# Expert weights and buffers laid over attention buffers in the order in which these die

## The reference

```python
# attention, per graph; 12 heads of 32
u = layernorm(x)
q, k, v = u @ Wq.T, u @ Wk.T, u @ Wv.T + bv
a = softmax(q @ k.T * 384**-0.5 + adj)            # rows that are all 0 are masked
x = x + (a @ v) @ Wo.T + bo
# experts, per graph; activations gelu, silu, mish, gelu
u = layernorm(x)
logits = u.mean(axis=1) @ router_w.T + router_b   # top 2 of 4, gates = softmax of the two
h = act_e(u @ w1[e] + b1[e])                      # 384 -> 768
y = sum(gate * (h @ w2[e] + b2[e])) + u
out = x + layernorm(y) * ln_g + ln_b
```

## Time and profile before

| | |
|---|---|
| median of 3 runs | 1660.82 us (1660.15 to 1662.0) |
| the profiled execution, its own time | 1659.58 us |
| its span, first to last instruction | 1657.8 us |
| PE busy | 1598.8 us, 96% |
| DVE, ACT, POOL busy | 71%, 58%, 50% |
| PE busy in the slices of 41 us from 663 and 705 us | 0.8 and 0.5 |
| DMA in the same two slices | 293 and 292 GB/s |

### The profile page before, as it was taken

One profiled execution on the slowest core, in us unless ns is written; L12 is line 12 of the kernel. 1 busy time (PEld: TensorE's weight loads), 2 busy tenths in 40 slices (PEclk: granted clock), 3 DMA queues, 4 the chain that ended last, 5 costly groups with the idle time before them and its releaser, 6 DMA issues.

```text
span 1657.8 us, 45212 instructions
## 1 busy us (share of the span) xinstructions
PE 1598.8 (96%) x12756; PEld 1533.7 (93%) x12757; DVE 1179.8 (71%) x3677; ACT 957.1 (58%) x2821; POOL 827.4 (50%) x1235
## 2 busy tenths in 40 slices
PE   8999999999999999859999999999999999999997
PEld 7999999999999999759999999999999999999997
DVE  5888888888888878737755665676677667566764
ACT  6899999999999988832422222333334323243431
POOL 4888888888888877612232333232323223322333
PEclk9999999999999999979999999999999999999999
DMA  6444443355555533872222222222221222222220
GB/s 194 144 141 140 133 141 128 136 173 171 179 178 172 175 127 124 293 292 63 63 73 72 71 72 72 72 72 72 72 72 57 64 71 70 72 72 72 72 69 33
DMA packets 93743, 188.19 MB, mean 114 GB/s; under 512 B 10336, under 2 KB 57440, under 8 KB 91872
## 3 DMA queue, kind: packets, MB, share of 16 engines
q1 hardware_dynamic: 91520, 169.39, 31.3%
q10 hardware_dynamic: 2016, 16.52, 2.7%
HBM read 108.80 MB, written 77.07 MB: 112 GB/s over the span
## 4 chain that ended last, share of the span: by engine, by line
PE 87%; DVE 5%; issue 3%; ACT 3%; POOL 1%; DMA 1%; DVEq 1%; ACTq 0%; POOLq 0%; SPq 0%
PE bank L423 67%; PE bank L497 5%; PE bank L622 4%; PE bank L450 3%; PE bank L520 3%; PE bank L537 2%; PE bank L529 1%; PE bank L506 1%; DVE half_t L1289 1%; DVE inverse L1296 1%; DVE inverse L1292 1%; ACT inverse L889 1%; ACT at_hi L856 1%; DMA ut_scratch<-ut_out 1%; DVE hid L1184 1%
## 5 line engine op out<-in xcount | busy, mean ns | idle before, releaser
L423 PE MATMUL bank<-w_hi,ut_in 128*128 x1536 | 423.8, 343 | 10.1 <-DVE hid L1184 8.9
L685 ACT ACTIVATE prob<-att,neg_max 128x128 f32<-128x128 f32 x768 | 297.3, 390 | 14.8 <-DVE neg_max L1044 11.2
L423 PEld LDWEIGHTS bank<-w_hi,ut_in 128*128 128x128 f32 x1536 | 281.5, 189 | 15.2 <-issue 15.0
L880 ACT ACTIVATE hid<-hid 128x384 f32<-128x384 f32 x192 | 95.1, 526 | 318.0 <-DVE hid L1184 305.2
L423 PE MATMUL bank<-w_hi,at_hi 128*128 x768 | 258.3, 336 | 5.0 <-DVE at_lo L1261 5.0
L1012 POOL TENSOR_SCALAR rs_z<-mv_z 128x1 f32<-128x1 f32 x64 | 14.7, 230 | 497.0 <-DVE mv_z L1315 450.0
L1261 DVE SCALAR_TENSOR_TENSOR at_lo<-bank,gate_col,at_hi 128x384 fp32r<-128x384 f32 x256 | 146.1, 612 | 162.9 <-ACT at_hi L856 162.9
L423 PE MATMUL bank<-w_lo,ut_in 128*128 x768 | 258.2, 336 | 0.0
L423 PE MATMUL bank<-w_hi,at_lo 128*128 x768 | 257.0, 335 | 0.0
L423 PE MATMUL bank<-w_lo,at_hi 128*128 x768 | 256.6, 334 | 0.0
L856 ACT ACTIVATE at_hi<-bank,gate_col 128x384 fp32r<-128x384 f32 x256 | 134.6, 577 | 170.0 <-PE bank L622 168.2
(11 more groups left out here) (135 smaller groups left out, 3826.5 us busy)
## 6 DMA issues: line engine op xcount, KB each, us to landing
xu_scratch<-xu SPq DMA_DIRECT2D x64, 384.0 KB, 2.3
ut_scratch<-ut_out SPq DMA_DIRECT2D x64, 384.0 KB, 2.7
ut_in<-ut_scratch SPq DMA_DIRECT2D x64, 384.0 KB, 3.0
xz<-xu_scratch SPq DMA_DIRECT2D x64, 384.0 KB, 3.1
x_in<-in_x SPq DMA_DIRECT2D x32, 384.0 KB, 4.9
xu<-in_x SPq DMA_DIRECT2D x32, 384.0 KB, 4.2
out_dram<-xz SPq DMA_DIRECT2D x64, 192.0 KB, 1.9
w_lo<-in_L_ffn_w SPq DMA_DIRECT2D x4, 1152.0 KB, 6.0
```

The lines of the kernel that those rows point to most:

```text
L423: last = nc.tensor.matmul(acc, lhs[c][a], rhs[c][b], start=start and n == 0, stop=stop and n == len(terms) - 1)
L685: nc.scalar.activation(prob[g][:, hh, :], att[g][:, head, :], ACT.Exp, bias=neg_max[g][:, head:head + 1], scale=-1.0, accum_out=row_sum[g] ...
L880: nc.scalar.activation(hid[k][:, s], hid[k][:, s], ACT.Gelu).then_inc(a_ready[k], 1)
```

## The change

SBUF is laid out anew. The attention buffers are allocated in an order in which those that die early lie under what is wanted early, and w2_lo and w2_hi become one region, w2_both, that lies exactly over a run of attention buffers: a filler, q and k of the even pairs, xt of the odd pairs, adj, q and k of the odd pairs, att0, prob0, att1, fold, prob1, pt, inv_t, inv_sum, and ot of both parities. The w2 scratch in HBM gets the same order within each partition, and eight transfers of unequal size take the place of eight equal ones of 2,304 columns. b1_wide and b2_wide change places in time: b1 is loaded in step 60 by ACT, and b2 only after attention, by SP, between the loads of xz0 and xz1.

Since other buffers now lie under hid, half_t, inverse and at_hi, the waits change too: ACT waits at the end of attention for the stores of xu0 and for the last output projection, no longer for the stores of xu1 and ut. DVE waits in step 65 for o_mm in place of xu_stored. And since b2 comes later, `add_output_bias` moves on DVE: for graph 0 to the end of (1, 0), for all other graphs to the end of their (b, k), behind `split_act_lo`, `activate_second` and `normalise_z`.

```diff
-    w2_dram = nc.dram_tensor("w2_scratch", (2, E, P, FC, D), F32, kind="Internal").ap()
+    w2_dram = nc.dram_tensor("w2_scratch", (P, 2, E, FC, D), F32, kind="Internal").ap()
...
-        w2_lo = sb("w2_lo", [P, E, FC, D], F32R)
-        w2_hi = sb("w2_hi", [P, E, FC, D], F32R)
         hid = [sb(f"hid{k}", [P, 2, HALF]) for k in range(K)]
-        half_t = sb("half_t", [P, 2, HALF])
+        w2_both = sb("w2_both", [P, 2, E, FC, D], F32R)
...
+        under = {}
+        edge = 0
+        for name, tiles in (("unused", (unused,)), ("qk0", (q_t[0], k_t[0])), ("xt1", (xt_hi[1], xt_lo[1])), ("adj", adj_in), ("qk1", (q_t[1], k_t[1])), ("att0", (att[0],)),
+                            ("prob0", (prob[0],)), ("att1", (att[1],)), ("fold", (fold,)), ("prob1", (prob[1],)),
+                            ("pt", pt), ("inv_t", (inv_t,)), ("inv_sum", inv_sum), ("ot0", (ot[0], ot_hi[0], ot_lo[0])),
+                            ("ot1", (ot[1], ot_hi[1], ot_lo[1]))):
+            width = sum(math.prod(tile[:].shape[1:]) for tile in tiles)
+            under[name] = (edge, edge + width)
+            edge += width
+        assert edge == 2 * E * FC * D
...
             load_xz(0, 0)
+            sp.dma_start(b2_wide[:].rearrange("p e d -> p (e d)"), b2.rearrange("(o e) d -> o (e d)", o=1).partition_broadcast(P)).then_inc(b2_loaded, 16)
             load_xz(1, 1)
...
-                            pe.wait_ge(w2_loaded, 32 * E)
+                            pe.wait_ge(w2_loaded, 16 * 8)
...
                 if h == B - 4:
                     act.wait_ge(xn_done, B)
-                    act.dma_start(b2_wide ...).then_inc(wide_loaded, 16)
+                    act.wait_ge(v_mm, B - 2)
                     act.wait_ge(qk_mm, 2 * B - 2)
+                    act.dma_start(b1_wide ...).then_inc(b1_loaded, 16)
                     load_w1_hi(1)
                 if h == B - 3:
                     act.wait_ge(qk_mm, 2 * B)
                     load_w1_hi(2)
+                    act.wait_ge(s_mm, B - 2)
+                    load_w2("unused", "qk0")
...
             def load_under_scores():
                 act.wait_ge(s_mm, B)
-                load_w2(0, 0)
                 act.wait_ge(exp_done, HEADS * (B - 1))
                 act.wait_ge(fold_done, FOLDS * (B - 1))
-                load_w2(0, 1)
+                act.wait_ge(pt_mm, PTC * (B - 1))
+                load_w2("qk1", "prob0")
...
             act.wait_ge(routed, 1)
             for g in range(2):
-                for p in range(2):
-                    act.wait_ge(xu_stored[p][g], 16 * (B // 4))
-                act.wait_ge(ut_stored[g], 16 * (B // 2))
+                act.wait_ge(xu_stored[0][g], 16 * (B // 4))
+            act.wait_ge(wo_mm, B)
...
                     if graph(b, 0):
                         activate_first(b, k, e)
-                        add_output_bias(b, k, m, lap, e)
...
                     if k == 0 and graph(b, -2):
                         normalise_z(b - 2, (m - 2) % 4)
+                    if isinstance(b, int) and (b, k) == (1, 0):
+                        dve.wait_ge(b2_loaded, 16)
+                        for first in range(K):
+                            add_output_bias(0, first, 0, 0, choice(0, first))
+                    if graph(b, 0) and not (isinstance(b, int) and b == 0):
+                        add_output_bias(b, k, m, lap, e)
```

113 lines of the change are left out of this document (60 added, 53 removed).

## The result

The changed kernel takes 1666.2 us in the median of 20 runs (1659.92 to 1670.76), the kernel before 1660.07 beside it (20 runs, 1657.37 to 1663.78). The ratio is 1.0032 with an interval from 1.0023 to 1.0041: slower, by a little over what can be told from no change. The profiled execution took 1666.42 us.

A forecast was written before the change was run, and what follows sets the result against it. PE, busy 96% of the span, was taken as the bound, losing time where attention ends. 13.8 - 2.2 - 5.4 = 6.2 us less: span 1651.6, median 1654.6; range 1648.5 to 1661.5 for 8 in 10.

The forecast's parts named there:

- The wait at the end of attention: ACT's first activation of the experts no longer waits for stores of ut and xu1: 12.2 us earlier.
- the residual load: Load of xu meets no w2 queue, so POOL's ot_lo of graph 62 starts earlier: gain 1.6 us, bounds 0 and 2.2.
- Weights in time: All of w2 lands near 727, before PE's first second_layer needs it at 732.6: cost 0.
- Output bias in step 1: Three biases on DVE between routing of (1, 0) and take of (1, 1): loss 2.2 us, from 1.3 to 3.2.
- Output bias in the other steps: Bias costs only at late takes, after 16 mish steps and at lap ends: 5.4 us, bounds 0 to 14.4.
- The second: Rival: none of the loop's output bias is hidden, at 16 mish takes and 14 laps; price 14.4, 1663.6 us; chance 0.13.
- The fourth: Rival: sequencer stalls move into late takes as lap code is reordered; up to 8 us, 1655 to 1663; chance 0.08.
- half the rate: By round robin between queues, the xu load would have half the rate, land within some 3 us, leaving 1.6 without cause.
- The term of 1.6 us: Gain at ot_lo of graph 62 from the xu load no longer queuing behind w2 loads near 697.

The follow-up runs named there:

- e7: Changed kernel with ScalarE's old waits for all eight stores of x and u put back ahead of the first activation; 1671.05 us.
- e3: Changed kernel with the output bias of graphs 2 to 63 just ahead of normalise_z in the first half step; 1654.05 us.
- e1: Changed kernel with the output bias of graphs 2 to 63 back at its old place, behind the first activation; 1648.38 us.
- e16: e1 plus one value_load on DVE in graph 1's second half step whose result nobody uses; 1653.67 us.
- e13: e8 with each copy of the gate made by a reduction over one element; 1653.43 us.
- e15: e1 with the first two portions of the second-layer weights issued behind the last scores, at some 691 us; 1648.88 us.
- e10: Changed kernel with each copy of the gate made by a reduction over one element at the same place; 1655.65 us.
- e4: Changed kernel with the gate copy for the second half step of graphs 2 to 63 made ahead of normalise_z, bias left in place; 1656.18 us.
- e8: e1 with the biases of graphs 0 and 1 spread: one after graph 1's first half step, three after its second; 1656.38 us.
- e12: e1 with each copy of the gate made by a reduction over one element; 1649.19 us.

## Why the prediction was wrong

Forecast were 1654.6 us and a gain; measured was 1666.2 and a loss. The profiled span is 1664.6 where 1651.6 was forecast: 1.3 of these 13.0 us arose ahead of graph 3 (10.3 gained there and not 11.6), and 11.7 in the loop, where the term was 5.4 and the rest lost 17.1.

- **The wait at the end of attention, and the residual load**: right in the mechanism, 1 to 2 us too high. Forecast 13.8 us earlier, measured 13.0 at ACT's activation and 12.0 at PE's first transposes; ot_lo of graph 62 was to start at 705.7 and starts at 705.60. SP's load of x started at 698.81, not near 697, and POOL still waits 1.3 us for it, at no cost. One sign did not come as written: no wait of PE was to exceed 3 us between 700 and 745, and it waits 4.6 us for ot_lo, which the same sentence had at 4.4, and 3.4 for the activation. That the wait was worth its time is shown by e7. Only half of the gain hangs on the waits alone, since the new order also lets the stores land sooner.
- **Weights in time**: right. No wait of PE for a transfer at the first second_layer.
- **Output bias in step 1**: right. Forecast a loss of 2.2 and a wait of 1.3. Measured on PE are 12.25 - 10.29 = 1.96 us and a wait of 1.69. (The wait was worked out from a row of the chain at 759.92; first_layer had begun at 759.68.)
- **Output bias in the other steps**: here it failed, and by its own sign: more than 10 us of new waits in the loop would be wrong, and PE's waits for hid grew by 21.1 - 8.1 = 13.0. The step read "a bias in between costs its pace, some 0.5. Six times, 3.0 us", and the whole term was 5.4. For the bias itself the term is right: 5.1 in e3, with 0.5 at each of the six places, and 5.7 between the medians of e1 and e3. But the term took for granted that what stands behind the bias keeps its duration. The copy of the gate came to lie under POOL's product, 0.98 us for 0.16, so that each of the six places cost 1.35, and the lap ends behind two of them 0.9 each (distances between PE's transposes in the two traces): 9.9 us with the clock left out, 15.6 with it, and the last 1.5 in small pieces where two mish steps follow each other and in second half steps. The range of this term, 0 to 14.4, counted the bias alone too; measured are 17.1. The trace of before had the sign: copies of up to 1027 ns beside a median of 170, and I did not ask what made them long.
- **The clock** had no term. PE's idle times of 1.8 and 3.3 us at the moved takes were followed by half clock, 5.7 us more than before by the chain. e7 isolates it: with the same code behind the waits and one fall of the clock in place of three, its rest is 6.4 us shorter. Without it the run would be about as long as before, 11.5 us lost in the loop and 10.3 gained ahead of it, and not 6.2 shorter.
- **Rivals.** The second (none of it hidden, 1663.6) has the sign and nearly the time, but not the mechanism: its price is 14.4 at 30 places, while without mish the price is zero. The fourth (stalls of the sequencers move) is not the cause here, since e1 and the kernel before have the same rest, yet it exists: 2.8 us by e16. The rule of the Trainium skill that the prediction set against its row (DMA: Bandwidth & Descriptors, section Queues, rings and completion order: each DMA engine goes round robin between the queues, packet by packet) agrees with the trace of e13, 178 packets of ACT's beside 174 of SP's, though such counts cannot tell turns of one packet from turns of several. What was wrong is what the prediction made of it, half the rate: the turns are even in packets, and SP's carried 0.27 MB beside 1.80. The row of before that the sum went by has both: from 698 to 700 SP's queue starts 1 packet and ACT's 95, and from 701 to 703 they start 86 and 77. So the order of arrival had a part in it, and turns had the rest. The term of 1.6 us is not what failed; ACT's last ut_out came 1.47 us earlier.

The best version is e1 or e15: 1648.4 to 1648.9, 0.7% under the kernel before and 1.1% under the changed one. The change was two edits, worth -11.7 and +17.8 us by the medians.

## What to carry to other kernels

Moving a short operation moves everything behind it: ask for each follower what runs beside it at its new time, on the other engines too. A duration whose maximum is six times its median is a question, not noise. And where a change consists of a gain and an edit that only makes room for it, the second needs its own measurement at the places without slack.

## What the runs showed of the hardware

- A DVE copy of 128x2 float32 numbers between on-chip buffers, begun under a GpSimd product of 128x384, ends only with it (0.16 us becomes 0.98), a reduction over one element at the same place does not (154 ns in the mean). Both directions show: an operation of DVE with two on-chip inputs, begun first, makes GpSimd's product 0.3 us longer (1312 ns in the mean, 1014 in e3). The Trainium skill (SBUF — State Buffer), on the shared port pair of DVE and GpSimd, says so in its section Who interferes with whom: an exclusive lock for the whole instruction, taken by fast-mode copies and by operations with two on-chip inputs. The traces agree, and they show that a copy of two columns is not too small for it.
- Single runs of the changed kernel go with the granted clock: 1659.92 us at a mean of 0.995, 1670.76 at 0.987. At 1471, after waits of 0.78 and 1.82 us, the granted clock was half (1.2 GHz); after waits of 0.78 and 0.46 us at the same half step of the kernel before it stayed full (2.4 GHz). It stayed full, too, after waits of 0.87 and 1.82 us at 810 of the changed kernel, so the waits alone do not tell.
- A value_load on DVE whose result nobody uses, ahead of a loop, makes the profiled rest 2.8 us longer (e16 beside e1), at the lap ends.
- Two queues of transfers share by packets and not by bytes: 174 packets of SP's with 0.27 MB beside 178 of ACT's with 1.80 MB in 5 us (e13). A load of 384 KB in packets of 1.5 KB took 4.4 us up to its use when it was started 0.37 us ahead of ACT's load (e1), 7.0 to 9.6 with a lead of 0.19 to 0.23 (e10, e4, e8, e12), and 12.1 when started 0.15 behind it (e13).
